# Loading the attention's and the experts' raw weights in the second to last chunk of the scan instead of the second one

## The chip, the cores and the metric

The kernel runs on one NeuronCore of one Trainium2 chip. The metric is the device time of one execution in microseconds (us); smaller is better. Where a time comes from the trace, it is counted from the first instruction of one profiled execution. The engines are named as the profile names them: PE (matmuls; PEld its weight loads), DVE (vector), ACT (scalar), POOL (GpSimd), and SP, which in this kernel does nothing but issue DMAs and wait for semaphores. SPq and ACTq are DMAs issued from SP and ACT.

## The reference

`x` has 32 sequences of 256 tokens of width 128, in float32. Four layers follow each other, each as `x = x + f(layernorm(x))`:

```
x = x + _L0_attn_a_ref(layernorm(x), ...)   # gated delta-rule scan over the 256 tokens, 16 heads of 8x8 state
x = x + _L0_ffn_ref(layernorm(x), ...)      # 8 experts, top 2 a token, hidden 512
x = x + _L0_attn_b_ref(layernorm(x), ...)   # causal softmax attention, 16 heads, low-rank score maps
x = x + _L0_ffn_ref(layernorm(x), ...)      # the same experts again
```

The scan is the layer that matters here. For each token, one after the other:

```
def step(state, inp):
    q_t, k_t, v_t, a_t, b_t = inp
    state = a_t[..., None, None] * state
    stored = jnp.einsum('bhij,bhj->bhi', state, k_t)
    delta = b_t[..., None] * (v_t - stored)
    state = state + jnp.einsum('bhi,bhj->bhij', delta, k_t)
    o_t = jnp.einsum('bhij,bhj->bhi', state, q_t)
    return (state, o_t)
```

`q`, `k`, `v`, `a`, `b` and the output gate are projections of layernorm(x); `o` is normalised, gated, projected with `Wout` and added to `x`.

## The kernel before, in words

`build` (L2258) runs four stages one after the other: `scan`, `ffn` (called ffn1), `attention`, `ffn` again (ffn2). Each stage is a block in which every engine has its own instruction stream; a block ends when all engines have ended it. Within a block the order on an engine is the order in which the code is written, and engines wait for each other only by semaphores.

**The scan** cuts the 256 tokens into 16 chunks of 16 tokens, numbered c = 2i + p with i from 0 to 7 and p 0 or 1. `run_chunks` (L183) writes chunks 0 and 1 out, then a hardware loop whose body is four chunks (chunks 2 to 13 in three turns), then chunks 14 and 15 written out again. In chunk c, DVE steps through 16 tokens (L717, L723, L726, L736 for each), and between these four instructions it does, at fixed slots, the preparation of chunk c+1 (`ahead`; it begins at slot 0 with `stats0`, L589, the first use of that chunk's x) and one transpose for chunk c-1 (`behind`). Buffers for x (`xin`) and for the residual rows (`xres`) are double.

**SP's queue** in chunk c (function `chunk`, L245) holds, in this order: the load of x for chunk c+1 (`load`, 4 DMAs, L218), which waits for DVE's last `xn` of chunk c-1; the load of the residual rows of chunk c (`load_res`, 4 DMAs, L225); the store of chunk c-1's result (`store`, 4 DMAs, L231), which waits for ACT's `x1` (step 14 of chunk c). So the store near the end of chunk c is directly followed by the x load for chunk c+2, whose first use is at the start of chunk c+1. In chunk 1, behind its store, stand `folding.loads` (L1542: `W_qkv`, `W_o`, the two low-rank maps and 16 small DMAs for `core`, L1549) and `raw.loads` (L801: `W1` and `W2` of the experts, 2 MB each). They are first used at the end of the scan, by `folding.keys_and_values` on DVE (L1597), and at the start of ffn1, by ACT (L857) and DVE (L877).

**The start of ffn1** (`setup_experts`, L807, and `ffn`, L893, share one block). SP issues the router's weights, `b1`, and `b2` spread over the partitions; then it waits until `b2` has landed (L827) and loads all of x1 into SBUF in 8 parts (L1027). ACT and DVE meanwhile split `W1` and `W2` into high and low float16 halves (L858, L878); then DVE begins layernorm (L1284, L1289, L1300).

Of the kernel before, what the change touches and what calls it, by code (L numbers as in the profile page):

```python
# [22 lines left out]
NC = T // TC  # L23
# [73 lines left out]
def scan(nc, ctx, A, ident, head_ones, bank, folding, raw):  # L97
# [3 lines left out]
    with ExitStack() as tmp:  # L101
# [73 lines left out]
        def prep_at(names, c, name):  # L175

            return c * len(names) + names.index(name) + 1

        def wait(eng, s, value):
            if not (isinstance(value, int) and value <= 0):  # L180
                eng.wait_ge(s, value)
# [12 lines left out]
        def ahead(i, p):  # L194

            if isinstance(i, int) and i == NC // 2 - 1 and p:
                return None
            return (i, 1) if p == 0 else (i + 1, 0)
# [12 lines left out]
        @block.sync  # L211
        def _(sp):
            def load(i, p):
                c = 2 * i + p

                wait(sp, prep_dve, prep_at(PREP, c - 2, "xn3") if not (isinstance(c, int) and c < 2) else 0)
                for l in range(4):
                    sp.dma_start(xin[p][32 * l:32 * l + 32, :, :], xc[c, l]).then_inc(x_in[p], 16)  # L218

            def load_res(i, p):  # L220
                c = 2 * i + p

                wait(sp, post_pe, prep_at(POST_PE, c - 2, "out") if not (isinstance(c, int) and c < 2) else 0)
                for l in range(4):
                    sp.dma_start(xres[p][32 * l:32 * l + 32, :, :], xc[c, l]).then_inc(x_res[p], 16)  # L225

            def store(i, p):
                c = 2 * i + p
                sp.wait_ge(post_act, prep_at(POST_ACT, c, "x1"))
                for l in range(4):  # L230
                    sp.dma_start(x1c[c, l], x1[p][32 * l:32 * l + 32, :, :]).then_inc(x1_out[p], 16)  # L231

            load(0, 0)
            sp.wait_ge(consts, 1)
            wabv = wab[:, :].rearrange("p (g r) -> p g r", g=HG)
            sp.dma_start(wabv[:, :, 0:HL], A["Walpha"].rearrange("e (g r) -> e g r", g=HG)).then_inc(weights, 16)
            sp.dma_start(wabv[:, :, HL:2 * HL], A["Wbeta"].rearrange("e (g r) -> e g r", g=HG)).then_inc(weights, 16)
            for dst, src in ((wk, "Wk"), (wq, "Wq"), (wv, "Wv"), (wg, "Wgate")):
                sp.dma_start(dst[:, :], A[src]).then_inc(weights, 16)
            load(0, 1)  # L240
            sp.dma_start(wout[:, :], A["Wout"]).then_inc(out_weights, 16)
            for hh in range(H):
                sp.dma_start(rmsw[D * hh:D * hh + D, :], A["rms_w"].rearrange("(p o) -> p o", o=1)).then_inc(out_weights, 16)

            def chunk(i, p):  # L245
                if ahead(i, p) and not (isinstance(i, int) and i == 0 and p == 0):
                    load(*ahead(i, p))
                load_res(i, p)
                if behind(i, p):
                    store(*behind(i, p))  # L250
                if isinstance(i, int) and i == 0 and p == 1:
                    folding.loads(sp)
                    raw.loads(sp)

            run_chunks(sp, chunk)
            store(NC // 2 - 1, 1)
            for p in range(2):
                sp.wait_ge(x1_out[p], 64 * (NC // 2))
# [548 lines left out]
def setup_experts(nc, ctx, sb, open_block, A, X, early, ident, bank):  # L807

    def sem(name):
        return ctx.enter_context(nc.semaphore(name))  # L810

    raw, raw_in = early.w, early.w_in
    biases = sb("biases", [NX * FC, P])
    iot = sb("iot", [P, NB + CB + NX], mybir.dt.int32)
    iot2 = sb("iot2", [P, P + NA + 2 * NT + 1 + NA], mybir.dt.int32)
    small_in, b2_in, high, low, masked, iotas, copied, turned = (
        sem(n) for n in ("small_in", "b2_in", "high", "low", "masked", "iotas", "copied", "turned"))

    block = open_block()

    @block.sync
    def _(sp):
        sp.dma_start(X.wgate[:, :], A["Wg"]).then_inc(small_in, 16)
        sp.dma_start(biases[:, :], A["b1"].rearrange("e (c p) -> (e c) p", c=FC)).then_inc(small_in, 16)
        sp.dma_start(X.b2[:, :, :].rearrange("p e d -> p (e d)"),
                     A["b2"].rearrange("e d -> (e d)").partition_broadcast(P)).then_inc(b2_in, 16)
        sp.wait_ge(b2_in, 16)  # L827

    @block.tensor
    def _(pe):  # L830
        pe.wait_ge(small_in, 16 * 2)
        n = NX * FC
        nc.tensor.transpose(bank[5][:, 0:n], biases[:, :], ident[0:n, 0:n]).then_inc(turned, 1)

    @block.gpsimd
    def _(pool):
        pool.memset(X.before[:, :], 1.0).then_inc(masked, 1)
        pool.memset(X.all16[:, :], 1.0).then_inc(masked, 1)
        pool.memset(X.onesrow[:, :], 1.0).then_inc(masked, 1)
        pool.wait_ge(masked, 3)  # L840

        pool.affine_select(out=X.before[:, :], in_=X.before[:, :], compare_op=ALU.is_gt, fill=0.0, base=0,
                           pattern=[[1, P]], channel_multiplier=-1).then_inc(masked, 1)
        pool.iota(iot[:, 0:NB], pattern=[[1, NB]], base=0, channel_multiplier=0).then_inc(iotas, 1)
        pool.iota(iot[:, NB:NB + CB], pattern=[[BS, CB]], base=0, channel_multiplier=0).then_inc(iotas, 1)
        pool.iota(iot[:, NB + CB:], pattern=[[1, NX]], base=-NX, channel_multiplier=0).then_inc(iotas, 1)
        pool.iota(iot2[:, 0:P], pattern=[[1, P]], base=0, channel_multiplier=0).then_inc(iotas, 1)
        pool.iota(iot2[:, P:P + NA], pattern=[[1, NA]], base=0, channel_multiplier=0).then_inc(iotas, 1)
        pool.iota(iot2[:, P + NA:P + NA + 2 * NT], pattern=[[1, 2 * NT]], base=1, channel_multiplier=0).then_inc(iotas, 1)
        pool.iota(iot2[:, P + NA + 2 * NT:P + NA + 2 * NT + 1], pattern=[[1, 1]], base=0,  # L850
                  channel_multiplier=1).then_inc(iotas, 1)
        pool.iota(iot2[:, P + NA + 2 * NT + 1:], pattern=[[P, NA]], base=2 * B * T, channel_multiplier=1).then_inc(iotas, 1)

    @block.scalar
    def _(act):
        for k, w in enumerate((X.w1, X.w2)):
            act.wait_ge(raw_in[k], 16)  # L857
            nc.scalar.activation(w[0][:, :, :, :].rearrange("p e c d -> p (e c d)"),  # L858
                                 raw[k][:, :, :].rearrange("p e f -> p (e f)"), ACT.Copy,
                                 scale=2.0 ** SPLIT).then_inc(high, 1)  # L860

    @block.vector
    def _(dve):
        dve.wait_ge(iotas, 8)
        nc.vector.tensor_copy(X.block_row[:, :], iot[:, 0:NB]).then_inc(copied, 1)
        nc.vector.tensor_copy(X.slot_row[:, :], iot[:, NB:NB + CB]).then_inc(copied, 1)
        nc.vector.tensor_copy(X.expert_m8[:, :], iot[:, NB + CB:]).then_inc(copied, 1)
        nc.vector.tensor_copy(X.slot_col[:, :], iot2[:, 0:P]).then_inc(copied, 1)
        nc.vector.tensor_copy(X.slot_tile[:, :], iot2[:, P:P + NA]).then_inc(copied, 1)
        nc.vector.tensor_copy(X.nth[:, :], iot2[:, P + NA:P + NA + 2 * NT]).then_inc(copied, 1)  # L870
        nc.vector.tensor_copy(X.row[:, :], iot2[:, P + NA + 2 * NT:P + NA + 2 * NT + 1]).then_inc(copied, 1)
        nc.vector.tensor_copy(X.spare[:, :], iot2[:, P + NA + 2 * NT + 1:]).then_inc(copied, 1)
        dve.wait_ge(turned, 1)
        nc.vector.tensor_scalar(X.b1[:, :, :].rearrange("p e c -> p (e c)"), bank[5][:, 0:NX * FC], 2.0 ** HSPLIT, None,
                                ALU.mult).then_inc(copied, 1)
        for k, w in enumerate((X.w1, X.w2)):
            dve.wait_ge(high, k + 1)  # L877
            nc.vector.scalar_tensor_tensor(w[1][:, :, :, :].rearrange("p e c d -> p (e c d)"),  # L878
                                           raw[k][:, :, :].rearrange("p e f -> p (e f)"), 2.0 ** SPLIT,
                                           w[0][:, :, :, :].rearrange("p e c d -> p (e c d)"),  # L880
                                           ALU.mult, ALU.subtract).then_inc(low, 1)
        dve.wait_ge(low, 2)
    return block


# [1424 lines left out]
```

## Time and profile before

| what | value |
|---|---|
| median of 3 runs | 2573.34 us (2571.94 to 2579.3) |
| the profiled execution's own time | 2566.48 us |
| its span, first to last instruction | 2564.7 us |
| busy: DVE, PE, ACT, POOL | 1918.4, 1759.5, 1444.0, 1386.8 us |
| mean granted clock of TensorE | 0.796 of full speed |
| moved by DMA | 122.01 MB, mean 48 GB/s |

The span is 40 slices of 64 us on the profile's page. The scan fills the first eleven and a bit (to 736 us), ffn1 the next seven, attention most of the following thirteen, ffn2 the rest. Busy shares are averages over stages with different limits, so what counts for a change is what is waited for at the place where it is made. In the timelines below a line is: start in us, duration in us, engine, line of the kernel, operation, output<-input with shapes, count, and in brackets how long the engine had been idle before and what ended that.

### The profile page before, as it was taken

To read this page: it belongs to the slowest core of one execution; us is meant where nothing else is said; L and a number is where in the kernel's file an instruction comes from. 1 tells how busy PE (TensorE), PEld (TensorE's weight loads), DVE (VectorE), ACT (ScalarE), POOL (GpSimd) and SP (SyncE) were. 2 spreads that over 40 slices of the span, in tenths; PEclk is the share of its full clock that TensorE was granted. 3 is DMA by queue.
4 is the path that set the end of the run, shared out by engine and by line. 5 is a ranking of instruction groups with operands and counts; after the bars stand their busy time and mean duration, and the time that the engine had idled before them with its cause. 6 is when DMAs were issued, how large, how long until landed. Compare 5 with 4: busy or idle time off the path is not lost. (4 is left out here: it accounts for less than half of the span.)

```text
span 2564.7 us, 59433 instructions
## 1 busy us (share of the span) xinstructions
PE 1759.5 (69%) x16780; PEld 1409.3 (55%) x16781; DVE 1918.4 (75%) x4981; ACT 1444.0 (56%) x3722; POOL 1386.8 (54%) x1511
## 2 busy tenths in 40 slices
PE   4556666666645589983888888888866467777671
PEld 2334444444434278871777777777766245555561
DVE  7689899999977867774898988898957943444346
ACT  5466676666632267761777777787762233443341
POOL 3445454445510055533788888888860056666661
PEclk8678777777765599995999999999985567777776
DMA  1200000000031023331121212211114011111117
GB/s 26 75 21 18 21 17 21 15 23 18 17 100 48 5 70 78 77 67 35 47 54 47 52 49 52 52 51 52 46 33 119 0 36 43 41 42 42 42 40 208
DMA packets 186755, 122.01 MB, mean 48 GB/s; under 512 B 23936, under 2 KB 175392, under 8 KB 186528
## 3 DMA queue, kind: packets, MB, share of 16 engines
q1 hardware_dynamic: 151328, 74.13, 10.6%
q0 software_dynamic: 17920, 36.74, 5.8%
q10 hardware_dynamic: 17280, 8.40, 1.1%
q8 instruction: 109, 1.79, 0.3%
q14 instruction: 118, 0.97, 0.1%
HBM read 66.22 MB, written 44.04 MB: 43 GB/s over the span
## 5 line engine op out<-in xcount | busy, mean ns | idle before, releaser
L1851 POOL TENSOR_TENSOR att_pl<-att_p,att_ph 128x384 f16<-128x384 f32 x512 | 463.1, 920 | 122.7 <-ACT att_ph L2071 112.7
L1067 POOL DMA_INDIRECT ffn_xs<-normed,ffn_tokeni x288 | 287.7, 999 | 447.0 <-DVE posi L1418 150.3
L326 POOL TENSOR_TENSOR sq<-states,qS 128x256 f32<-128x256 f32 x256 | 243.2, 950 | 349.6 <-DVE states L736 308.2
L1251 ACT ACTIVATE ffn_h<-bank,b_cols 128x256 f32<-128x256 f32 x576 | 230.0, 474 | 326.4 <-remote 202.6
L546 ACT ACTIVATE decayed<-states,alpha 128x64 f32<-128x64 f32 x1024 | 272.2, 336 | 215.9 <-DVE states L736 214.6
L2165 DVE TENSOR_REDUCE att_mx<-bank 128x3 f32<-128x384 f32 x512 | 277.7, 551 | 59.2 <-PE bank L1912 53.9
L382 PE MATMUL bank<-sq,ident 128*128 128x128 f32 x1024 | 249.8, 415 | 101.9 <-POOL sq L326 101.9
L2068 ACT ACTIVATE att_p<-bank 128x384 f32<-128x384 f32 x512 | 252.7, 493 | 118.6 <-PE bank L1945 106.2
L382 PEld LDWEIGHTS bank<-sq,ident 128*128 128x128 f32 x1024 | 219.8, 239 | 135.9 <-POOL sq L326 109.2
L1174 PE MATMUL bank<-w_h,ffn_hh 128*128 x1152 | 245.0, 238 | 58.8 <-issue 34.0
L1174 PE MATMUL bank<-w_l,ffn_hh 128*128 x1152 | 243.8, 238 | 22.8 <-issue 22.5
L1174 PE MATMUL bank<-w_h,ffn_hl 128*128 x1152 | 243.5, 237 | 21.3 <-issue 21.1
L2071 ACT ACTIVATE att_ph<-bank 128x384 f16<-128x384 f32 x512 | 252.4, 493 | 0.0
L1442 DVE TENSOR_TENSOR ffn_hl<-ffn_h,ffn_hh 128x512 f16<-128x512 f32 x288 | 201.9, 701 | 8.1 <-ACT ffn_hh L1260 1.0
L1073 POOL DMA_INDIRECT picked<-ffn_ys,ffn_targeti x144 | 149.4, 1038 | 105.0 <-DVE ffn_ys L1451 71.2
L1161 PE MATMUL bank<-ffn_xl,w_h 128*128 128x256 f16 x576 | 175.3, 304 | 13.4 <-issue 13.2
L1960 PEld LDWEIGHTS bank<-att_vx,att_ph 128*128 128x128 f16 x3072 | 179.1, 97 | 8.3 <-POOL att_pl L1851 1.9
L1161 PE MATMUL bank<-ffn_xh,w_l 128*128 128x256 f16 x576 | 174.9, 304 | 12.6 <-issue 12.4
L1911 PE MATMUL bank<-att_kp,att_qz 128*128 128x256 f16 (+1 forms) x1024 | 172.5, 251 | 15.3 <-DVE att_mx L2165 14.2
L1161 PE MATMUL bank<-ffn_xh,w_h 128*128 128x256 f16 x576 | 176.2, 306 | 5.8 <-issue 5.7
L1960 PE MATMUL bank<-att_vx,att_ph 128*128 128x9 f16 x3072 | 178.5, 168 | 1.6 <-POOL att_pl L1851 1.6
L1451 DVE SCALAR_TENSOR_TENSOR ffn_ys<-bank,b_rows 128x256 f32<-128x256 f32 x144 | 60.3, 419 | 150.5 <-DMA normed<-ffn_xn 142.1
(336 smaller groups left out, 5306.5 us busy)
## 6 DMA issues: line engine op xcount, KB each, us to landing
slots<-ffn_ys SPq DMA_DIRECT2D x72, 128.0 KB
ffn_x_all<-x SPq DMA_DIRECT2D x16, 512.0 KB, 4.7
normed<-ffn_xn ACTq DMA_DIRECT2D x32, 256.0 KB, 2.3
att_qz<-att_qp SPq DMA_DIRECT2D x256, 32.0 KB
ffn_yg<-picked SPq DMA_DIRECT2D x32, 256.0 KB, 4.6
ffn_xs<-normed,ffn_tokeni POOLq DMA_INDIRECT x288
xin<-in_x SPq DMA_DIRECT2D x64, 64.0 KB, 1.9
xres<-in_x SPq DMA_DIRECT2D x64, 64.0 KB, 2.0
```

What stands on the lines that cost most here:

```text
L326: nc.gpsimd.tensor_tensor(sq[:, t, :].rearrange("p (h i j) -> p h i j", h=HL, i=D), states[:, t, :].rearrange("p (h i j) -> p h i j", h=HL ...
L382: ins = nc.tensor.matmul(ps_a[:, P * n:P * n + P], ident[:, :], sv[:, :, j], start=(j == 0), stop=(j == D - 1))
L546: ins = nc.scalar.activation(decayed[:, 64 * h:64 * h + 64], states[:, (t - 1) % TC, 64 * h:64 * h + 64], ACT.Copy, scale=alpha[p][:, t, h ...
L1067: pool.indirect_dma_start(xs[j % AHEAD][:, r, :], None, A["normed"], bass.IndirectOffsetOnAxis(ap=tokeni[:, BR * j + r:BR * j + r + 1], ax ...
L1161: ins = nc.tensor.matmul(o, X.w1[w][:, bass.ds(e, 1), c, :].rearrange("p o d -> p (o d)"), x[b][:, :], start=(n == 0), stop=(n == 2))
L1174: ins = nc.tensor.matmul(ps_y[b][:, P * r:P * r + P], h[b][:, c, P * r:P * r + P], X.w2[w][:, bass.ds(e, 1), c, :].rearrange("p o d -> p ( ...
L1251: nc.scalar.activation(h32[b][:, c, :], bank[2 + 2 * b + c // 2][:, BS * (c % 2):BS * (c % 2) + BS], ACT.Relu, bias=X.b1[:, bass.ds(e, 1), c],
L1851: nc.gpsimd.tensor_tensor(pl[:, h % RP, :], p32[:, h % RP, :], ph[:, h % RP, :], ALU.subtract).then_inc(low_done, 1)
L1960: ins = mm(ps_y[p % 2][:, at_y:at_y + D + 1], pt[:, h % RP, o:o + P], vx[p][:, s, h, a, :], start=(n == 0), stop=(n == len(todo) - 1))
L2068: a(p32[:, h % RP, :], ps_st[h % 2][:, 0:SW], ACT.Exp, scale=2.0 ** (-2 * AS)).then_inc(exp_done, 1)
L2071: a(ph[:, h % RP, :], ps_st[h % 2][:, 0:SW], ACT.Exp, scale=2.0 ** (-2 * AS)).then_inc(high_done, 1)
L2165: v.tensor_reduce(mx[p % 2][:, h, :], ps_s[h % 2][:, 0:SW].rearrange("p (a n) -> p a n", n=P), AX_X, ALU.max).then_inc(max_done, 1)
```

## The change

Three edits.

1. The two calls `folding.loads(sp)` and `raw.loads(sp)` move from chunk 1 to chunk 14, again behind the store that stands there. They are not behind any x load of a later chunk then: the last one, for chunk 15, is issued at the top of chunk 14.
2. The load of chunk 15's residual rows, which stood at the top of chunk 15, is written just ahead of them, at the end of chunk 14.
3. In `setup_experts`, SP no longer waits for `b2` to land; DVE waits for it instead, behind the last instruction of its part there.

```diff
             def chunk(i, p):
                 if ahead(i, p) and not (isinstance(i, int) and i == 0 and p == 0):
                     load(*ahead(i, p))
-                load_res(i, p)
+                if not (isinstance(i, int) and i == NC // 2 - 1 and p == 1):
+                    load_res(i, p)
                 if behind(i, p):
                     store(*behind(i, p))
-                if isinstance(i, int) and i == 0 and p == 1:
+                if isinstance(i, int) and i == NC // 2 - 1 and p == 0:
+                    load_res(i, 1)
                     folding.loads(sp)
                     raw.loads(sp)
...
         sp.dma_start(X.b2[:, :, :].rearrange("p e d -> p (e d)"),
                      A["b2"].rearrange("e d -> (e d)").partition_broadcast(P)).then_inc(b2_in, 16)
-        sp.wait_ge(b2_in, 16)
...
         dve.wait_ge(low, 2)
+        dve.wait_ge(b2_in, 16)
```

On SP, between the store of chunk 0's result in chunk 1 and the branch into the loop (x_0 is the result buffer of even chunks, x_1 that of odd ones):

```order
 L225 DMA xres<-in_x 32x4x128 x4
 L231 DMA x<-x_0 32x4x128 x4
-L1544 DMA wqkv<-in_W_qkv 128x384
-L1545 DMA wo<-in_W_o 128x128
-L1546 DMA lq<-in_W_q_lsr 128x32
-L1547 DMA lk<-in_W_k_lsr 128x32
-L1549 DMA core<-in_core 8x32 x16
-L802 DMA raw_w<-in_W 128x8x512
-L803 DMA raw_w<-in_W 128x32x128
 L187 UNCONDITIONAL_BRANCH
```

The 22 DMAs that stood between the store and the loop, whose first DMAs are the x load for chunk 3 (buffer xin1), are gone from there.

On SP, from the store of chunk 13's result, near the end of chunk 14, to that of chunk 14's result (line numbers are two higher in the new file):

```order
 L231 DMA x<-x_1 32x4x128 x4
 L225 DMA xres<-in_x 32x4x128 x4
+L1546 DMA wqkv<-in_W_qkv 128x384
+L1547 DMA wo<-in_W_o 128x128
+L1548 DMA lq<-in_W_q_lsr 128x32
+L1549 DMA lk<-in_W_k_lsr 128x32
+L1551 DMA core<-in_core 8x32 x16
+L804 DMA raw_w<-in_W 128x8x512
+L805 DMA raw_w<-in_W 128x32x128
 L231 DMA x<-x_0 32x4x128 x4
```

They now stand between the last residual load and the store of chunk 14's result. The residual load keeps its place in SP's queue: it was directly behind this store before, too.

## Rows read from the trace of the kernel before

**Rows 1.** Stretch by windows: us, busy PE PEld DVE ACT POOL, PEclk, DMA share, GB/s.

```profile
200.00:240.00 40.00, 25.54 (x86) 17.41 (x85) 37.00 (x101) 26.61 (x85) 19.68 (x21) 0.74 0.08 20
```

**Rows 2.** Waits of the stretch 120 to 150 us: total, times, longest.

```profile
DVE st L589 <- DMA xin<-in_x: 21.9, 1, 21.9
```

**Rows 3.** Timeline of SP's queue, 100 to 130 us.

```profile
104.42 1.79 SPq L231 DMA_DIRECT2D x<-x  x4
106.26 0.45 SPq L1544 DMA_DIRECT2D wqkv<-in_W_qkv  x1
...
113.65 0.41 SPq L802 DMA_DIRECT2D raw_w<-in_W  x1
114.27 0.78 SPq L803 DMA_DIRECT2D raw_w<-in_W  x1
116.02 11.20 SPq L218 DMA_DIRECT2D xin<-in_x  x4
```

**Rows 4.** Timeline of DVE: the instruction behind its longest wait.

```profile
131.32 0.29 DVE L589 BATCH_NORM_STATS2 st<-xin 128x6 f32<-128x128 f32 x1 [21.87 <-DMA xin<-in_x]
```

**Rows 5.** Two windows of 2 us while the weights land.

```profile
116.00:118.00 2.00, 0.00 (x0) 0.00 (x0) 0.00 (x0) 0.00 (x0) 0.00 (x0) 0.50 1.02 370
...
130.00:132.00 2.00, 0.00 (x0) 0.00 (x0) 0.68 (x3) 0.00 (x0) 0.00 (x0) 0.50 0.48 93
```

**Rows 6.** Timelines of SP and DVE at the start of chunk 3.

```profile
170.44 1.85 SPq L218 DMA_DIRECT2D xin<-in_x  x4
...
173.87 0.29 DVE L589 BATCH_NORM_STATS2 st<-xin 128x6 f32<-128x128 f32 x1 [0.53 <-DMA xin<-in_x]
```

**Rows 7.** Timeline of SP's queue at the end of chunks 14 and 15.

```profile
679.30 1.79 SPq L231 DMA_DIRECT2D x<-x  x4
681.14 2.36 SPq L225 DMA_DIRECT2D xres<-in_x  x4
714.28 21.04 SPq L231 DMA_DIRECT2D x<-x  x8
```

**Rows 8.** DMAs of 112 to 131 us: KB a descriptor, us to landing (the line of W2).

```profile
raw_w<-in_W SPq DMA_DIRECT2D x1, 0.5 KB, 15.8
```

**Rows 9.** Timeline: first users of the moved loads, and DVE's layernorm behind them.

```profile
716.33 0.18 DVE L1599 SCALAR_TENSOR_TENSOR lq<-lq,core 128x32 f32<-128x32 f32 x1
737.15 7.12 ACT L858 ACTIVATE w_h<-raw_w 128x4096 f16<-128x4096 f32 x2 [3.63 <-PEq L101]
...
749.87 0.87 DVE L1284 BATCH_NORM_STATS2 ffn_st<-ffn_x_all 128x6 f32<-128x128 f32 x4 [0.30 <-DVE w_l L878]
```

**Rows 10.** The page's DMA line: packets, bytes and rate over the whole span.

```profile
DMA packets 186755, 122.01 MB, mean 48 GB/s; under 512 B 23936, under 2 KB 175392, under 8 KB 186528
```

**Rows 11.** Line L736 over the span: duration min/median/max in ns.

```profile
L736 DVE TENSOR_TENSOR states<-decayed,outer x256: 358/425/1375, 30.2 to 716.0; 128x256 f32<-128x256 f32 x128
```

**Rows 12.** Line L1284 in 742 to 762 us, then in 764 to 800 us.

```profile
L1284 DVE BATCH_NORM_STATS2 ffn_st<-ffn_x_all x20: 260/276/294, 749.9 to 760.9; 128x6 f32<-128x128 f32 x12, 128x6 f32 x8
L1284 DVE BATCH_NORM_STATS2 ffn_st<-ffn_x_all x44: 272/277/296, 763.9 to 795.6; 128x6 f32 x40, 128x6 f32<-128x128 f32 x4
```

**Rows 13.** A window of 4 us while x1 is loaded.

```profile
754.00:758.00 4.00, 2.81 (x15) 2.41 (x13) 2.86 (x18) 1.96 (x6) 0.00 (x0) 0.50 0.89 249
```

**Rows 14.** DMAs of 691 to 709 us: queue, kind, packets, MB, share.

```profile
q8 instruction: 1, 0.02, 0.5%
```

**Rows 15.** Timeline of ffn1's start: SP's queue and a wait of DVE.

```profile
738.03 0.41 SPq L825 DMA_DIRECT2D b_rows<-in_b  x1
741.98 15.76 SPq L1027 DMA_DIRECT2D ffn_x_all<-x  x8
...
759.23 1.11 DVE L1300 TENSOR_SCALAR ffn_xn<-ffn_x_all,ffn_mv,ffn_rstd 128x128 f32 x4 [2.07 <-DMA normed<-ffn_xn]
```

**Rows 16.** Turn of the loop (SP, DVE), 296 to 310 us.

```profile
297.96 2.00 SPq L218 DMA_DIRECT2D xin<-in_x  x4
302.30 0.28 DVE L589 BATCH_NORM_STATS2 st<-xin 128x6 f32<-128x128 f32 x1
```

## The prediction

> **What bounds the kernel now.** I read the page's slices first, to place the stages. The change touches the scan and the first microseconds of ffn1, so all else is read there. Then windows over the scan. In an undisturbed stretch DVE is busy 37.00 of 40 us [rows 1], PE and ACT about 26, POOL less than 20, the DMA engines 8%. The recurrence on DVE bounds the scan, and a microsecond in which DVE stands still is a microsecond of the kernel, because no stage overlaps the next.
>
> Next the waits of DVE, the only engine whose waits cost anything there. One stands out: at the start of chunk 2 it waits 21.9 us, once, for a DMA of x [rows 2]. The timelines show why. SP issues the store of chunk 0 at 104.42, then the 20 loads of `folding`, then `W1` at 113.65 and `W2` at 114.27, and only then the x load that chunk 2 wants, at 116.02; those four DMAs take 11.20 us to issue where four others take 1.8 [rows 3]. DVE starts at 131.32 after 21.87 us of waiting, so it was ready at 109.45 [rows 4]. Meanwhile all engines stand at 0.00 busy, the DMA engines are full at 370 GB/s, and the flood ends in the window 130 to 132, where DVE begins again [rows 5]. So this wait is caused by the moved loads alone.
>
> **Edit 1, what goes.** Without the 22 DMAs, the x load comes directly behind the store. SP has the store issued at 106.21 (104.42 + 1.79). From the end of `W2`'s issue (115.05) to the x load it took 0.97 us, with the loop's entry in it; taking the same, the load starts at 107.18. How long such a load takes until DVE starts on it is read one chunk later: issue at 170.44, `stats0` at 173.87, with DVE already waiting, 3.43 us [rows 6]. That gives 110.61, so a wait of 1.16 us stays and 131.32 - 110.61 = 20.7 us go. The bounds: 21.87 if nothing is left to wait for; and a little less than 20.7 if something else was hidden in the pause. I looked for that: after it, chunk 2 takes 173.87 - 131.32 = 42.55 us from `stats0` to `stats0`, and the three chunks behind it take (302.30 - 173.87) / 3 = 42.81 each, a turn of the loop among them [rows 4, 6, 16]. So chunk 2 had no advantage of the pause in which PE, ACT and POOL caught up. What might be hidden is an engine's jump into the loop body. The turn of the loop shows its price: there the x load takes from 297.96 to 302.30 until DVE uses it, 4.34 instead of 3.43 us [rows 6, 16]. That is 0.91 us for SP, and I allow the same for DVE. Lower bound 20.7 - 1.8 = 18.9, upper 21.9; I take 20.7, from the nearest rows.
>
> **Edit 1, what comes.** In chunk 14 SP issues the store at 679.30 and the residual load from 681.14 to 683.50 [rows 7]. Nothing is queued behind the new loads but the store of chunk 14, ready at 714.28 [rows 7], since there is no x load any more. The 20 `folding` DMAs take 113.65 - 106.26 = 7.4 us to issue [rows 3], so `W1` goes out at 690.9 and `W2` at 691.5. `W2` landed 15.8 us after its issue [rows 8]: 707.3, on the old clock (everything here comes 20.7 us earlier, needs and loads alike). Who needs what: DVE the attention's weights at 716.33, which are ahead of `W1` in the queue and so there by about 693; ACT `W1` at 737.15 [rows 9]; SP the free queue at 714.28. The margins are 23, 30 and 7 us. The loads are hidden beneath chunk 15, which DVE ends just before 716.33. Their cost on this path: 0.
>
> That cover has a price if DMA traffic slows the engines. The trace shows DVE's layernorm under both conditions: a BN_STATS takes 276 ns in the median while x1 pours in, at 249 GB/s in the window shown, and 277 ns afterwards [rows 12, 13]. The recurrence itself never ran beside 370 GB/s in this trace, as everything stood still then. The nearest row for a disturbed step is the worst of its own instructions: L736 takes 425 ns in the median and 1375 at most [rows 11]. From token 14 of chunk 14 to that of chunk 15 SP's stores are 714.28 - 679.30 = 35.0 us apart [rows 7], 2.2 us a token, so 17 us of flood hold eight, and 8 x 0.95 = 7.6 us is the upper bound. Below nothing it can't go, as a transfer doesn't make an instruction shorter. I take 0, by rows 12, the only ones with the same engine under both conditions.
>
> A second thing shares the DMA engines: the engines' own instruction fetch. In what will be the flood's time the trace has one such packet [rows 14]; chunk 15 is written out code and must be fetched. If such a fetch stood behind all that SP has queued, it would wait up to 17 us. The nearest that the rows have is a DMA of x that came behind the flood, but on the same queue [rows 3]. The queue of the fetches is another (q8, SP's is q1).
> The Trainium skill ("DMA: Bandwidth & Descriptors", Queues, rings and completion order) says that a DMA engine goes round its queues packet by packet; by that a fetch loses a packet's time, not the queue's, and the term is 0. The Trainium skill ("Runtime: NRT & Kernel Launch", Instruction fetch mechanics) adds that an engine fetches its next block while it executes the present one. No row here shows a fetch delayed or not; by queueing behind everything the term would be up to 17 us. Both weigh only on how likely the rival below is.
>
> **Edit 2** changes nothing in SP's order: the last residual load followed this store before as well. 0.
>
> **Edit 3.** SP issues `b2` until 738.44 and the first part of x1 only at 741.98 [rows 15]; without the wait the load starts some 3.5 us earlier. But DVE begins layernorm at 749.87, right behind its own `w_l` [rows 9], which hangs on ACT's work from 737.15 on, not on x1. So the start doesn't move. Where it can help is DVE's wait of 2.07 us for a store of `normed` that shares the DMA engines with x1's parts [rows 15]. That store is issued before 759 while x1 is still coming, with or without 3.5 us of lead, so I count 0.3 us of it; bounds 0 and 2.1. DVE's new wait is for a DMA issued more than 11 us before DVE gets there and costs 0; behind it stands all of DVE's layernorm, so a late `b2` would cost its lateness.
>
> **Sum.** 20.7 + 0 + 0 + 0.3 = 21.0 us. The profiled execution took 2566.48 us, so 2545.5 for one like it. The median of the runs lies 6.9 us above that execution (2573.34), and I put the difference on the median: 2552.3 us, which is 0.8% less. A measurement of this kernel can tell about 0.3%, 7.7 us, from no change.
>
> **The rivals.**
> A. The loads are not free in chunk 15: steps slow beside the flood, or a fetch is late. For it: no row shows the recurrence under 370 GB/s. Against it: rows 12, and the separate queue. With half the bound of 7.6 us the gain is 17.2 and the time 2556.1; with all of it 2559.9, still faster.
>
> B. The wait only moves, within 0.3% of before. A fetch that stands behind the whole flood stops an engine in chunk 15 and the recurrence with it: 17 us of the 21.0 go back, 2569.3 us. For it: the flood fills all 16 DMA engines for 15 us and more, with the fetch needed in that time. Against it: only one packet falls into it, from an engine's look ahead, and the queue is another.
>
> C. Slower: the experts' weights come too late. It is the one term without a ceiling, since ACT's first instruction of ffn1 and DVE's layernorm behind it wait for `W1` and `W2`. It decides once they land after 737.15, 46 us after their issue, and it eats the whole gain when they land at 758.2, at 67 us, or 63 GB/s for 4.2 MB. If beside running engines the loads got only the kernel's mean rate, 48 GB/s [rows 10], they would take 87 us, land at 778, and cost 41 us: 2552.3 + 41 = 2593 us. For it: that they must share with compute now, where before all stood still. Against it: x1's parts, of the same size together, ran at 249 GB/s beside a working DVE [rows 13].
>
> **Chances and range.** The forecast 0.83; A 0.10; B 0.03; C 0.02; 0.02 for what I don't see, half of it near no change. Faster thus 0.94, within 0.3% 0.04, slower 0.02. The bounds of the forecast itself: gain 18.9 to 24.0 (21.9 + 2.1), 2549.3 to 2554.4 on the median. To this come the spread of the runs (2571.94 to 2579.3 before, and the profiled one lower still, by which the median could come out near 2545.5), and A upward to 2559.9, with 1 us for the lower bound of what goes. Range 2544 to 2561.
>
> **What would show it.** In the profile after: DVE's wait at the second chunk's end falls from 21.87 to about 1.2 us, and SP's x load is issued near 107 in 1.8 us. The scan ends, by ACT's first `w_h`, at 737.15 - 20.7 = 716.5. A burst of 300 to 400 GB/s stands at about 670 to 688 with DVE at 90% busy or more in it, where the trace before has next to nothing. SP's store of chunk 14 takes 1.8 us for four DMAs, not 11. The x1 load follows `b2` at once, and DVE's layernorm still begins 12.7 us behind the first `w_h`. All later stages keep their lengths. I am wrong if L736 or L717 grow in the burst (A), if one engine stands for over 10 us in chunk 15 (B), if ACT waits for `raw_w` (C), or if the first wait of DVE in chunk 2 goes to another releaser at more than 4 us.

## The result, and the profile after

The changed kernel took 2547.59 us (median of 5 runs, 2545.34 to 2556.78), the kernel before on the same chip 2571.94 (5 runs, 2567.34 to 2579.3). The ratio is 0.9909, with a 95% interval of 0.9883 to 0.9934: faster by 0.9%, and clear of the 0.3% that such a measurement can tell. The forecast was 2552.3, in a range of 2544 to 2561. The profiled execution took 2547.59 us where the one before took 2566.48.

The page after begins with these two lines:

```profile
span 2545.8 us, 59433 instructions
...
GB/s 26 13 14 26 14 25 13 26 13 25 84 119 26 16 78 77 77 58 35 50 53 52 51 49 51 48 52 51 45 49 104 0 38 44 41 41 41 41 42 209
```

The 75 GB/s of the second slice are gone, and the eleventh has 84 where it had 17: the 4 MB have moved.

SP's queue and DVE at the start of chunk 2, in the timeline after:

```profile
105.44 1.79 SPq L231 DMA_DIRECT2D x<-x  x4
107.72 1.86 SPq L218 DMA_DIRECT2D xin<-in_x  x4
...
111.23 0.29 DVE L591 BATCH_NORM_STATS2 st<-xin 128x6 f32<-128x128 f32 x1 [0.77 <-DMA xin<-in_x]
```

The x load follows the store and is issued in 1.86 us, not 11.20. DVE waits 0.77 us for it, not 21.87 [rows 3, 4]. It starts on x at 111.23 and not at 131.32; the times around it are 1.0 us late in this trace, since DVE began the recurrence that much later in this execution (29.64 against 28.59). From its first L717 to being ready for this x DVE took 80.82 us, and 80.86 before.

The end of chunk 14 and what follows, on all queues, in the timeline after:

```profile
659.55 1.79 SPq L231 DMA_DIRECT2D x<-x  x4
661.38 1.93 SPq L225 DMA_DIRECT2D xres<-in_x  x4
...
670.92 0.41 SPq L804 DMA_DIRECT2D raw_w<-in_W  x1
671.53 0.83 SPq L805 DMA_DIRECT2D raw_w<-in_W  x1
...
694.53 19.78 SPq L231 DMA_DIRECT2D x<-x  x8
...
696.57 0.18 DVE L1601 SCALAR_TENSOR_TENSOR lq<-lq,core 128x32 f32<-128x32 f32 x1
...
716.16 7.12 ACT L859 ACTIVATE w_h<-raw_w 128x4096 f16<-128x4096 f32 x2 [3.65 <-PEq L101]
717.49 17.37 SPq L1029 DMA_DIRECT2D ffn_x_all<-x  x8
...
728.87 0.87 DVE L1286 BATCH_NORM_STATS2 ffn_st<-ffn_x_all 128x6 f32<-128x128 f32 x4 [0.30 <-DVE w_l L879]
738.23 1.11 DVE L1302 TENSOR_SCALAR ffn_xn<-ffn_x_all,ffn_mv,ffn_rstd 128x128 f32 x4 [2.06 <-DMA normed<-ffn_xn]
```

The two stores stand 694.53 - 659.55 = 34.98 us apart with the 4 MB between them, and 34.98 without [rows 7]. ACT begins ffn1 at 716.16, 21.0 us before 737.15 [rows 9]. DVE's last token is only 19.8 us earlier (`lq<-lq` at 696.57, before at 716.33 [rows 9]); the other 1.2 us lie behind it, in the tail of the scan, which took 19.6 us from `lq<-lq` to the first `w_h`, and 20.8 before. PE's clock makes them. Five microseconds of the tail, before and after (columns as in rows 1):

```profile
721.00:726.00 5.00, 3.72 (x9) 1.39 (x7) 2.45 (x12) 1.57 (x3) 0.00 (x0) 0.50 0.00 0
```

```profile
701.00:706.00 5.00, 2.96 (x12) 1.48 (x11) 3.25 (x17) 1.95 (x3) 0.17 (x1) 0.99 0.00 0
```

The granted clock there was 0.50 (1.2 GHz) before and 0.99 (nearly all of it at 2.4 GHz) after, and PE's two matmuls on `osq` took 2.04 and 1.10 us. In five traces of later runs the tail took 20.8 to 20.9 us, at 0.50 in the same place, and two of these had all loads in chunk 14 (`e2_loads_only` and the changed kernel again). So these 1.2 us are no effect of the change. x1's load now follows `b2` at once (717.02 + 0.42), but layernorm still begins 12.7 us behind the first `w_h`, and its wait for `normed` is 2.06 us where it was 2.07 [rows 9, 15].

Four windows of 4 us while the weights land, in chunk 15 (columns as in rows 1):

```profile
670.00:674.00 4.00, 0.00 (x0) 0.00 (x0) 3.76 (x10) 2.13 (x8) 1.93 (x2) 0.50 0.45 120
674.00:678.00 4.00, 1.99 (x3) 0.99 (x4) 3.70 (x9) 2.65 (x9) 1.93 (x2) 0.50 0.99 367
678.00:682.00 4.00, 4.00 (x19) 3.88 (x18) 3.72 (x9) 2.96 (x11) 2.15 (x3) 0.67 1.05 316
682.00:686.00 4.00, 3.52 (x16) 2.75 (x14) 3.76 (x8) 2.39 (x9) 3.10 (x3) 1.00 0.92 251
```

DVE is busy 3.7 to 3.8 of each 4 us, in the last three beside DMA engines that are 0.92 to 1.05 busy. No step of the recurrence grew: over the 25 us in which the flood lies, L738 takes 424 to 1369 ns with a median of 426, and its counterpart L736 in the same place before takes the same; L719 takes 425 ns both times. The instruction fetches that fell into 660 to 700 us (one of the four, q8's, into the flood of 671 to 687), and three rows from the waits of that stretch:

```profile
q8 instruction: 1, 0.02, 0.2%
q14 instruction: 3, 0.02, 0.2%
```

```profile
POOL sq L328 <- DVE states L738: 15.5, 18, 1.4
ACT decayed L548 <- DVE states L738: 15.2, 17, 1.8
PEld bank L391 <- ACT osq L522: 7.6, 1, 7.6
```

POOL's and ACT's waits for DVE are the usual ones of the recurrence, 1.8 us at most. PE waits longer, 7.6 us at most, but for ACT, and the trace before has the same 7.6 us in the same place. No wait is new, so no sign is left of a fetch that held an engine up.

### The profile page after: what moved, and what is told of

Same layout as the page of the kernel before. It is cut to its first block and busy times, and to the rows that moved or that the text cites. A ratio compares the mean times of both kernels' runs of the same rounds, so it can differ in the third digit from the quotient of the medians.

```text
span 2545.8 us, 59433 instructions
## 1 busy us (share of the span) xinstructions
PE 1757.3 (69%) x16780; PEld 1408.6 (55%) x16781; DVE 1920.4 (75%) x4981; ACT 1443.5 (57%) x3722; POOL 1386.0 (54%) x1511
## 5 line engine op out<-in xcount | busy, mean ns | idle before, releaser
L1176 PE MATMUL bank<-w_l,ffn_hh 128*128 x1152 | 242.8, 237 | 21.6 <-issue 21.6
```

The lines of the kernel that those rows point to most:

```text
L1176: ins = nc.tensor.matmul(ps_y[b][:, P * r:P * r + P], h[b][:, c, P * r:P * r + P], X.w2[w][:, bass.ds(e, 1), c, :].rearrange("p o d -> p ( ...
```

## Experiments

The first eight ran on one chip, four and four together (kernel before there: 2558.13 us in 13 runs, then 2557.15 in 11). `e9_no_loop` and the changed kernel again ran on a second chip (2457.08, 9 runs), the last experiment on a third (2452.95, 9 runs). The level differs from chip to chip; so across them only ratios and the scan's own times, which hardly differ, are compared. "First `w_h`" is ACT's first instruction of ffn1 (716.16 after, 737.15 before): it marks the scan's end, give or take the 1.2 us of the tail's clock. Where that matters, the text gives the scan on DVE: from the first L717 to `lq<-lq`, 687.7 us before and 666.9 after.

**Edit 3 alone** (`e1_b2_only`)

```diff
-        sp.wait_ge(b2_in, 16)
...
+        dve.wait_ge(b2_in, 16)
```

> The kernel before with edit 3 alone (DVE waits for b2 instead of SP). My theory: x1's load starts about 3.5 us earlier (right behind b2 instead of 3.5 us later), but DVE's layernorm still begins 12.7 us behind ACT's first w_h and its wait for normed stays at 2.07 us, so the time is that of before, ratio 1.000, and the profile's stage boundaries don't move. Rival: the lead of x1's load is worth its 3.5 us, ratio 0.9986, with layernorm beginning 9.2 us behind w_h.

Measured: ratio 0.9989 (0.9973 to 1.0006). From its timeline:

```profile
738.07 7.12 ACT L857 ACTIVATE w_h<-raw_w 128x4096 f16<-128x4096 f32 x2 [3.64 <-PEq L101]
...
739.39 5.95 SPq L1027 DMA_DIRECT2D ffn_x_all<-x  x3
...
750.78 0.87 DVE L1284 BATCH_NORM_STATS2 ffn_st<-ffn_x_all 128x6 f32<-128x128 f32 x4 [0.30 <-DVE w_l L877]
```

x1's load starts 1.3 us behind `w_h` and not 4.8, and layernorm begins 12.7 us behind it as before. The lead is spent on nothing, because DVE's own `w_l` ends last there. The wait for `normed`, which I had expected to stay at 2.07 us, is 3.15 us here; with and without edit 3 it lies anywhere from 2.06 to 3.15 us. The interval leaves room for up to 2.7 parts in a thousand, but no row has them.

**Edits 1 and 2 alone** (`e2_loads_only`)

```diff
         sp.dma_start(X.b2[...], ...).then_inc(b2_in, 16)
+        sp.wait_ge(b2_in, 16)
...
-        dve.wait_ge(b2_in, 16)
```

(against the changed kernel)

> The kernel before with edits 1 and 2 alone (loads in chunk 14; SP still waits for b2). My theory: the whole gain is here, ratio 0.991 as in the changed kernel, first w_h at 716.1 us instead of 737.15, and DVE's wait for x at the start of chunk 2 about 1 us. Rival: part of the 24 us between the medians comes from edit 3; then this one keeps at most 21 us less that part.

Measured: ratio 0.9907 (0.9878 to 0.9936), first `w_h` at 716.29, DVE's wait for x 0.7 us. All of the gain that the runs can tell is here.

**Only the experts' weights moved** (`e3_attention_stays`) and **only the attention's moved** (`e4_experts_stay`)

```diff
                 if isinstance(i, int) and i == NC // 2 - 1 and p == 0:
                     load_res(i, 1)
-                    folding.loads(sp)
                     raw.loads(sp)
+                if isinstance(i, int) and i == 0 and p == 1:
+                    folding.loads(sp)
```

and the same with `raw.loads` in place of `folding.loads`.

> The changed kernel, but the 20 loads for the attention (folding.loads) stay in chunk 1 behind the store; only W1 and W2 are moved. My theory: the wait had two parts that add, SP's issue time of the small loads and the transfer of the big ones. Here only the issue time of 7.4 us is left: x is issued at about 114.6, DVE starts on it at about 118, a wait of 8 to 9 us, first w_h at about 723.7. Rival: only the flood of 4 MB held x up, the small loads fit in SP's idle time: wait 1 us, w_h at 716.

> The changed kernel, but W1 and W2 stay in chunk 1 behind the store; only the 20 attention loads are moved. My theory: x is issued at about 108.6 and queues behind the 4 MB, which now start 7.4 us earlier than in the kernel before: DVE starts at about 124 instead of 131.3, a wait of 14 to 15 us, first w_h at about 729.5; with the run that leaves the attention loads in chunk 1 the two waits above the usual 1 us add up to the 20.7 that were lost. Rival: the flood alone makes the whole wait, 21 us, or x slips past it because the queue serves its DMAs in turn, wait below 5 us.

The x load and its first use, first with the 20 attention loads left in chunk 1:

```profile
115.16 1.92 SPq L218 DMA_DIRECT2D xin<-in_x  x4
118.65 0.30 DVE L592 BATCH_NORM_STATS2 st<-xin 128x6 f32<-128x128 f32 x1 [8.60 <-DMA xin<-in_x]
```

then with `W1` and `W2` left there:

```profile
108.58 11.91 SPq L218 DMA_DIRECT2D xin<-in_x  x4
124.33 0.29 DVE L592 BATCH_NORM_STATS2 st<-xin 128x6 f32<-128x128 f32 x1 [14.48 <-DMA xin<-in_x]
```

The waits are 8.60 and 14.48 us. Above the 0.77 that stays they are 7.8 and 13.7, together 21.5; the kernel before had 21.87 - 0.77 = 21.1. So the wait had two parts, one behind the other: SP was busy issuing small DMAs (x is issued late, in 1.9 us), then x stood in the queue behind 4 MB (issued early, but in 11.9 us). First `w_h` at 724.57 and 730.67, one execution each, both with the slow tail of 20.8 us. In `e2_loads_only`, with both groups moved, 0.7 us of waiting are left.

**All loads in the scan's first microseconds** (`e5_before_store`)

```diff
-                if not (isinstance(i, int) and i == NC // 2 - 1 and p == 1):
-                    load_res(i, p)
+                load_res(i, p)
+                if isinstance(i, int) and i == 0 and p == 1:
+                    folding.loads(sp)
+                    raw.loads(sp)
                 if behind(i, p):
                     store(*behind(i, p))
-                if isinstance(i, int) and i == NC // 2 - 1 and p == 0:
-                    load_res(i, 1)
-                    folding.loads(sp)
-                    raw.loads(sp)
```

> The changed kernel, but all 22 loads stay in chunk 1, ahead of the store instead of behind it. My theory: what matters is not the stage but whether the queue is free when the next x load is due. Here the loads go out from about 70 us on, W2 has landed at about 95, ten us before the store at 104.4 and the x load behind it: DVE's wait at the start of chunk 2 stays near 1 us and the time is that of the changed kernel, ratio to before 0.991. Rival: the loads are cheap only in the last chunk, where no preparation of a next chunk runs; beside chunk 1's preparation the 4 MB cost up to 7.6 us (the prediction's bound for eight disturbed tokens), or x still comes late, and the ratio is 0.994 or more.

I had the place wrong: nothing ahead of the loads makes SP wait in chunk 1, so they went out still earlier, beside chunk 0:

```profile
21.63 0.43 SPq L1544 DMA_DIRECT2D wqkv<-in_W_qkv  x1
...
28.98 0.41 SPq L802 DMA_DIRECT2D raw_w<-in_W  x1
```

```profile
34.00:38.00 4.00, 0.00 (x0) 0.00 (x0) 3.86 (x11) 2.12 (x9) 1.56 (x2) 0.50 1.02 354
```

Chunk 0, from its first L717 to the next `stats0`, took 68.42 - 29.61 = 38.8 us as before (67.38 - 28.59), at 354 GB/s beside it. DVE's wait in chunk 2 was 1.2 us. Ratio 0.993 (0.9902 to 0.9958), first `w_h` at 718.18: 2.0 us later than after. Of these 1.2 us are the tail, here at a clock of 0.50; the scan on DVE took 667.7 us, 0.8 more than after and within what the other looped kernels without the long wait took (666.5 to 667.7). The ratio alone doesn't part the two theories; chunk 0's length and the wait do, since chunk 0 too carries the preparation of a next chunk.

**One chunk later** (`e6_last_chunk`)

```diff
-                if isinstance(i, int) and i == NC // 2 - 1 and p == 0:
-                    load_res(i, 1)
+                if isinstance(i, int) and i == NC // 2 - 1 and p == 1:
                     folding.loads(sp)
                     raw.loads(sp)
```

> The changed kernel, but the 22 loads come one chunk later, behind the store of chunk 14 (about 694.5 us on the changed kernel's clock). My theory: the margins are used up. The attention's loads have landed at about 705.5 instead of before 696.6, DVE's first instruction on them waits some 9 us and its transpose for chunk 15 stands behind it; W2 lands at about 719.5 and the last store behind it. First w_h at about 725 instead of 716.1, 9 us more. Rival: the loads are hidden there as well (x1's last store and the block's end cover them), first w_h within 1 us of 716.

```profile
704.28 0.19 DVE L1599 SCALAR_TENSOR_TENSOR lq<-lq,core 128x32 f32<-128x32 f32 x1 [8.04 <-DMA core<-in_core]
...
723.39 7.12 ACT L857 ACTIVATE w_h<-raw_w 128x4096 f16<-128x4096 f32 x2 [3.70 <-PEq L101]
```

DVE waits 8.04 us for `core`, and first `w_h` is 7.2 us late, in one execution; the expected 9 were a little too many. The cover behind which the loads are free ends here.

**The flood three times** (`e7_thrice`)

```diff
-                    raw.loads(sp)
+                    for n in range(3):
+                        raw.loads(sp)
+                        if n < 2:
+                            sp.wait_ge(raw.w_in[0], 16 * (n + 1))
+                            sp.wait_ge(raw.w_in[1], 16 * (n + 1))
...
-            act.wait_ge(raw_in[k], 16)
+            act.wait_ge(raw_in[k], 48)
```

> The changed kernel, but W1 and W2 are loaded three times over into the same buffers, each time once the one before has landed: the DMA engines are full for some 50 us of chunk 15 and behind it instead of 17. My theory: the recurrence doesn't feel it (DVE reaches its first instruction behind the last token, lq<-lq, at 696.6 as in the changed kernel, 33 us after the residual load), but the third transfer ends near 723, the stores of chunks 14 and 15 land behind it, and first w_h is at about 725 to 727, 10 us more than 716.1. Rival A of the prediction (the flood slows the recurrence): DVE reaches lq<-lq later, by up to 0.95 us for each token beside a flood, 10 us and more over chunk 15.

```profile
660.51 1.79 SPq L231 DMA_DIRECT2D x<-x  x4
...
671.85 0.41 SPq L808 DMA_DIRECT2D raw_w<-in_W  x1
...
687.86 0.40 SPq L808 DMA_DIRECT2D raw_w<-in_W  x1
...
704.02 0.37 SPq L808 DMA_DIRECT2D raw_w<-in_W  x1
...
697.53 0.18 DVE L1605 SCALAR_TENSOR_TENSOR lq<-lq,core 128x32 f32<-128x32 f32 x1
722.11 7.12 ACT L863 ACTIVATE w_h<-raw_w 128x4096 f16<-128x4096 f32 x2 [7.38 <-PEq L101]
```

From the store at chunk 14's end to `lq<-lq` DVE took 697.53 - 660.51 = 37.02 us; in the changed kernel 696.57 - 659.55 = 37.02. The second flood began at 687.86, beside the last 9.7 us of the recurrence, the third at 704.02, behind it. So the floods ran on to the recurrence's end, and cost it nothing that a hundredth of a microsecond shows: rival A falls. The first two rounds took 16.0 and 16.2 us instead of the 17 that I had counted, so the last ended near 720. First `w_h` is 5.95 us later than after, not 10, and not all of that is the third flood: 1.0 us had been lost before chunk 14, and this tail ran at a clock of 0.50. Against another tail at that clock (20.8 us) this one, of 24.6, is 3.7 us longer, and ACT's wait ahead of `w_h` grew by as much, from 3.65 to 7.38. It is one execution.

**x ahead of the store** (`e8_x_first`)

```diff
-                if ahead(i, p) and not (isinstance(i, int) and i == 0 and p == 0):
-                    load(*ahead(i, p))
                 if not (isinstance(i, int) and i == NC // 2 - 1 and p == 1):
                     load_res(i, p)
+                if not (isinstance(i, int) and i == NC // 2 - 1):
+                    load(i + 1, p)
                 if behind(i, p):
                     store(*behind(i, p))
```

> The changed kernel, with one thing more: in every chunk c of the scan SP issues the x load for chunk c+2 ahead of the store of chunk c-1 and not behind it (it waits only for a buffer that has been free since chunk c-1), so that x has landed long before it is wanted. My theory: DVE's remaining waits for x at the start of chunks, 5.1 us in 11 places in the changed kernel's profile, go, and nothing takes their place, so the scan ends about 5 us earlier, first w_h at 711, ratio to before about 0.989 instead of 0.991. Rival: the wait moves to the next thing that is late at a chunk's start (POOL's gate product, ACT's decay), first w_h stays at 716 within 1 us.

Measured: ratio 0.9912 (0.9895 to 0.9929), first `w_h` at 715.63. DVE waits for x no more (5.1 us before, 0 now), and 0.5 us came of it: my theory fell. The rival was right that the time stays, if not in how: it had the wait move to another releaser, and what the last pair shows is an instruction that grows.

**The loop written out** (`e9_no_loop`), and with it **the changed kernel again**

```diff
-            with eng.Fori(0, (NC // 2 - 2) // 2) as two:
-                for u in range(2):
-                    for p in range(2):
-                        chunk(two * 2 + (1 + u), p)
+            for i in range(1, NC // 2 - 1):
+                for p in range(2):
+                    chunk(i, p)
```

> The changed kernel with the scan's loop written out: chunks 2 to 13 stand one after the other, no turn of a loop. In the changed kernel chunks follow each other in 42.3 us, but 45.2 and 44.3 us where the loop turns. My theory, the one behind the prediction's lower bound: the turn itself costs these 2 to 3 us, so two turns' 4.9 us go, the first w_h comes at about 711 and no chunk takes over 43 us. Rival: the longer code must be fetched all the way and stops engines elsewhere; then the chunks grow or single ones stand out, and w_h stays at 716 or comes later.

> The changed kernel once more, beside the other runs of this chip. My theory: the ratio to before is 0.991 again, with first w_h at 716 within 1 us, since 21.0 us of the difference are in the scan and the stages behind it are those of before; what the first medians showed above that (24.35 us) is scatter between runs. Rival: the later stages gain as well, 3 us, and ratio and profile show it again.

Measured: 2417.69 us, ratio 0.9843 (0.9825 to 0.9861); the changed kernel 2430.51, ratio 0.9892 (0.987 to 0.9913). First `w_h` at 699.52 and 717.04, the scan on DVE 649.9 and 667.4 us. From one SP store to the next, in us (the changed kernel from its first trace, after):

| chunk | 2 | 3 | 4 | 5 | 6 | 7 | 8 | 9 | 10 | 11 | 12 | 13 | 14 |
|---|---|---|---|---|---|---|---|---|---|---|---|---|---|
| changed kernel | 42.75 | 42.47 | 41.91 | 42.33 | 45.18 | 42.06 | 42.43 | 42.29 | 44.33 | 42.39 | 42.37 | 42.08 | 41.52 |
| loop written out | 41.05 | 41.71 | 41.51 | 41.47 | 41.34 | 41.5 | 41.32 | 41.15 | 41.07 | 41.04 | 41.0 | 41.68 | 41.33 |

The two turns cost 2.9 and 2.0 us above their neighbours, as I had read. But each of the other chunks in the loop is 1 us slower than written out as well (42.3 against 41.3 in the mean of ten), so 17.5 us of the scan went and not 5. The medians are only 12.8 us apart and the profiled spans 21.0, which says how far times of the whole kernel can be trusted beside those of the scan. Chunk 14, written out in both, stands at 41.52 and 41.33. What in the loop body costs this microsecond wasn't taken apart.

Of the changed kernel's second measurement my theory was that the difference to before stays at the scan's 21.0 us. It is 26.6 us by the medians, at least 21.4 by the interval, so the rival (the later stages gain too) isn't refuted.

**Both** (`e10_no_loop_x_first`, the two diffs above together)

> Both additions together: the scan's loop written out, and the x load for chunk c+2 ahead of the store of chunk c-1. Written out, chunks take 41.3 us, and DVE still waits 12.7 us in 13 places for x. Theory: with the loop gone DVE has nothing else to wait for at a chunk's start, so most of these 12.7 us go; first w_h at 689 to 692 instead of 699.5, ratio to before about 0.981 instead of 0.984. Rival: as in the looped version, where 5.1 us of such waits were taken away and 0 to 1 us came of it, DVE's instructions grow by what its waits lose (they share a read path with POOL, whose product of the same token then falls beside them): first w_h within 3 us of 699.5, ratio 0.984.

Measured: 2411.98 us, ratio 0.9829 (0.981 to 0.9849), first `w_h` at 697.80: 1.7 us of the 12.7 (1.4 in the scan on DVE). The interval overlaps that of the loop written out alone, so the times don't show this version as the faster one. Groups of DVE instructions between 108 and 618 us, busy and mean ns, then idle before them; the loop written out:

```profile
L727 DVE TENSOR_TENSOR outer<-delta,kS 128x256 f32<-128x256 f32 x199 | 108.2, 544 | 2.6
...
L590 DVE BATCH_NORM_STATS2 st<-xin 128x6 f32<-128x128 f32 x52 | 14.9, 286 | 12.7 <-DMA xin<-in_x 12.7
```

and both changes:

```profile
L727 DVE TENSOR_TENSOR outer<-delta,kS 128x256 f32<-128x256 f32 x199 | 121.1, 608 | 2.6
...
L590 DVE BATCH_NORM_STATS2 st<-xin 128x6 f32<-128x128 f32 x52 | 14.7, 282 | 0.0
```

12.7 us of waiting became 12.9 us of a longer `outer`. (Between the same times of the looped pair `outer` grew from 104.1 to 107.4 us while 4.4 us of waiting went.) The timeline of one chunk's start shows how. With the wait, POOL's gate product fell into it:

```profile
192.77 1.26 POOL L282 TENSOR_TENSOR gE<-gR,gsig 128x512 f32<-128x512 f32 x1
...
193.33 0.29 DVE L590 BATCH_NORM_STATS2 st<-xin 128x6 f32<-128x128 f32 x1 [1.10 <-DMA xin<-in_x]
...
194.09 0.41 DVE L727 TENSOR_TENSOR outer<-delta,kS 128x256 f32<-128x256 f32 x1
```

Without it:

```profile
192.27 1.27 POOL L282 TENSOR_TENSOR gE<-gR,gsig 128x512 f32<-128x512 f32 x1
192.39 1.42 DVE L727 TENSOR_TENSOR outer<-delta,kS 128x256 f32<-128x256 f32 x1
```

`outer` now begins 0.12 us behind the product, takes 1.42 us instead of 0.41, and ends 0.27 us behind the product's end. The Trainium skill ("SBUF — State Buffer", Who interferes with whom) says that a DVE instruction with two SBUF inputs and a GpSimd instruction that reads SBUF exclude each other, and the one that comes second waits; by that rule, this trace agrees. A full wait would have put the end 0.41 us behind the product's, which it misses by 0.14 us. The wait for x had not been free time: POOL's instruction hid in it.

## Why the prediction was right

**What goes.** The step counted 20.7 us for the wait. DVE's own wait fell by 21.87 - 0.77 = 21.1, first `w_h` by 21.0. The x load was issued 2.28 us behind the store's start where I had put 2.76, and used 3.51 us later where I had put 3.43. The scan on DVE, from the first L717 to `lq<-lq`, became 687.7 - 666.9 = 20.8 us shorter. That first `w_h` moved by just the 21.0 of the sum is partly luck: the recurrence began 1.05 us later in this execution, and the tail was 1.2 us shorter by PE's clock. The two halves that `e3` and `e4` take apart add up, and with both moved (`e2`) the wait is 0.7 us, which shows that it was all due to the moved loads.

**What comes.** The step put the loads at 0, hidden beneath chunk 15. The stores on both sides of the flood are 34.98 us apart either way, and floods up to the recurrence's end left it at 37.02 us. That part was argued before from BN_STATS alone [rows 12]; now it is shown for the recurrence. The margins were right in kind: a chunk later they are gone (8.04 us of waiting), and thrice the bytes lengthen the tail by 3.7 us. `W2` took 15.0 us to land instead of 15.8.

**Edit 2** cost nothing; the residual load keeps its place. **Edit 3** I gave 0.3 us of the 2.07 us wait for `normed`; the wait is 2.06 after and 3.15 with edit 3 alone, and no run shows the term to be other than 0. It was the one term set without a row that spoke for it.

**The rivals.** A (steps slow beside the flood) is refuted by `e5` and `e7`. B (a fetch behind the flood): four fetch packets fell into 660 to 700 us, one of them into the flood itself, and no engine had a wait that the trace before doesn't have too. By the rule of the Trainium skill that I had set beside it ("DMA: Bandwidth & Descriptors", Queues, rings and completion order: the DMA engines serve their queues in turn), the trace agrees, as far as one packet can. C (weights too late) did not occur; `e6` and `e7` show where it would.

**The size.** The terms gave 21.0 us, the scan on DVE 20.8; the medians differ by 24.35, the profiled executions by 18.9. Both differences hold something from behind the scan: in the profile after, attention begins 21.6 us earlier, and the last layer's last BN_STATS comes 19.7 us earlier (1950.6 against 1970.3). Scatter of the later stages is big enough for that. From first `w_h` to attention's first instruction (`att_eps`) it took 420.3 us before and 419.6 after, but 424.2 in `e1_b2_only`, which in ffn1 had 30 us at a granted clock of 0.92 where the others have 1.00. Against pure scatter speaks that the medians gave more than the scan's 21 us each time the change was measured: 24.4, 23.4 (`e2_loads_only`) and 26.6 us. So whether the later stages gain some 3 us stays open; no experiment was made on them. The forecast itself needs only the 21.

**What was not right** is a side reading. I took the turn of the loop as the only price of the loop and used twice 0.91 us as a bound. `e9` shows that a turn costs 2 to 3 us, and each chunk in the loop another one. The bound held for a reason that I had not read: what DVE needs to enter the loop lies ahead of its wait for x, with the loads in either place (80.86 and 80.82 us from the first L717 until it is ready for x, 80.07 with the loop written out), so the pause hid nothing of it. Entering the loop costs DVE 0.8 us by these numbers.

## What to carry to other kernels

A queue that both feeds a critical loop and carries bulk loads has room for them only where nothing that is due soon stands behind them: look for the place by what the queue must deliver next, and count both the issue time of small DMAs and the transfer of large ones, since they add. Loads from SP cost a running DVE nothing here, at up to 367 GB/s, so only the next use and the next transfer on the queue set the place. Before taking a small wait away, look at what another engine does in it: what hid there can come out again as a longer instruction.

A marker such as the first instruction of the next stage can move by a microsecond for reasons of its own. Measure a term of this size on the engine that it is about, from its own first to its own last instruction.

## What the runs showed of the hardware that I had not expected

- The kernel before took 2557 to 2572 us in three measurements and 2453 to 2457 us on two other chips. The changed kernel's spans differ likewise (2545.8 and 2433.8 us) with the scan's end at nearly the same time (716.16 and 717.04): the 112 us lie in the later stages only. In the stretch 900 to 1000 us PE was busy 92.25 us with 1115 matmuls in the first of these traces and 99.95 us with 1284 in the second, both at a granted clock of 1.00. The cause wasn't looked for.
- The same tail of the scan took 19.6 us with PE's granted clock at 0.99 in five of its microseconds and 20.8 to 20.9 us with it at 0.50, in the same program.
- Written out, the scan's chunks take 41.0 to 41.7 us; in a loop of four chunks 42.3, and 44.3 to 45.2 at a turn. The written out code, with 240 fetch packets instead of 228 in the whole kernel, stopped no chunk noticeably.
- A DVE instruction that began 0.12 us behind one of POOL took 1.42 us instead of 0.41 and ended 0.27 us behind it.
